# Moving the expert choice of a decoder layer's router behind slot six's row maximum, and its prefix count to slot eight

## The reference, cut to what matters

```python
x = layernorm(x + mixer(x))          # gated causal convolution with a linear scan over time
x = layernorm(x + attention(x, ctx)) # cross attention, 16 heads of 16 dims
x = layernorm(x + experts(x))        # top-1 router, 8 experts, capacity 640
# in experts, over all 4096 tokens t:
probs = softmax(t @ Wr);  idx = argmax(probs);  pmax = max(probs)
onehot = one_hot(idx, 8)
pos = sum(cumsum(onehot, axis=0) * onehot, -1) - 1
kept = pos < 640
flat = idx * 640 + minimum(pos, 639)
# kept tokens go to row `flat` of their expert's block, through relu(. @ W1) @ W2,
# and are scaled by pmax; the others stay as they are
```

## Time and profile before

| | |
|---|---|
| median of 3 runs | 869.91 us (869.25 to 873.31) |
| profiled execution | 871.27 us, span 869.5 us |
| TensorE matmul busy | 800.4 us, 92% |
| VectorE busy | 609.1 us, 70% |
| ScalarE busy | 400.6 us, 46% |
| GpSimd busy | 353.1 us, 41% |
| slices of the span at 0.9 or more of TensorE's full clock | 34 of 40 |

### The profile page before, as it was taken

How to read it: one execution, slowest core, us unless ns; L and a number is a source line. 1 busy time by engine, 2 the same in 40 slices (tenths; PEclk the granted TensorE clock), 3 DMA queues, 4 the chain that set the end, 5 groups by cost and what they waited for, 6 DMA issues and landing times. The chain is left out here.

```text
span 869.5 us, 16600 instructions
## 1 busy us (share of the span) xinstructions
PE 800.4 (92%) x5754; PEld 628.8 (72%) x5754; DVE 609.1 (70%) x1456; ACT 400.6 (46%) x644; POOL 353.1 (41%) x292
## 2 busy tenths in 40 slices
PE   8998987889998999999999999885899999999995
PEld 6776765556666767676666666544899999999994
DVE  5889883455788888888888887645266666666754
ACT  5665652135555655555655556452334234423420
POOL 1332442323255444455544453215331454255335
PEclk9999998689999999999999999897899999999999
DMA  4101931454454445465445444131512432343201
GB/s 135 49 27 48 289 106 45 140 152 130 123 169 154 115 148 159 137 172 156 124 135 174 125 143 147 56 116 44 169 51 91 129 120 86 107 146 98 79 1 49
DMA packets 76081, 100.93 MB, mean 116 GB/s; under 512 B 11065, under 2 KB 63522, under 8 KB 76024
## 3 DMA queue, kind: packets, MB, share of 16 engines
q1 hardware_dynamic: 72568, 92.06, 35.2%
q0 software_dynamic: 3456, 8.13, 2.6%
HBM read 65.47 MB, written 35.74 MB: 116 GB/s over the span
## 5 line engine op out<-in xcount | busy, mean ns | idle before, releaser
L1303 DVE TENSOR_REDUCE nmax<-ps_m 128x4 f32<-128x1024 f32 x128 | 156.6, 1224 | 49.7 <-PE ps_m L881 41.8
L1101 ACT ACTIVATE pt<-ps_a 128x1024 f32<-128x1024 f32 x128 | 131.8, 1030 | 76.6 <-PE ps_a L891 51.9
L1576 ACT ACTIVATE hid<-ps_h 128x640 fp32r<-128x640 f32 x64 | 45.2, 706 | 147.1 <-PE ps_h L1504 147.1
L1504 PE MATMUL ps_h<-xt,w_hi 128*128 128x320 f32 x512 | 101.5, 321 | 1.0 <-DVE xt L1591 1.0
L1686 POOL DMA_INDIRECT out_rows<-gated,token x40 | 50.2, 1254 | 91.4 <-issue 91.4
L1641 DVE SCALAR_TENSOR_TENSOR hid<-ps_h,hid 128x640 fp32r<-128x640 f32 x64 | 52.8, 825 | 49.2 <-ACT hid L1576 48.7
L881 PE MATMUL ps_m<-kst,qst 48*128 48x256 f32 x512 | 66.4, 338 | 19.8 <-DVE nmax L1303 15.8
L757 POOL TENSOR_TENSOR half<-kq,half 128x512 fp32r<-128x512 f32 x32 | 41.7, 1302 | 103.2 <-ACT half L1067 103.2
L1504 PEld LDWEIGHTS ps_h<-xt,w_hi 128*128 128x128 f32 x512 | 80.6, 193 | 4.1 <-DVE hid L1641 2.8
L1518 PE MATMUL ps_y<-w,hid 128*128 128x512 f32 x320 | 80.3, 393 | 0.8 <-DVE gated L1659 0.8
L881 PEld LDWEIGHTS ps_m<-kst,qst 48*128 48x128 f32 x512 | 39.6, 191 | 52.8 <-issue 25.8
(11 more groups left out here) (211 smaller groups left out, 1617.2 us busy)
## 6 DMA issues: line engine op xcount, KB each, us to landing
halves_dram<-half SPq DMA_DIRECT2D x64, 256.0 KB, 2.5
gated<-in_w SPq DMA_DIRECT2D x16, 1024.0 KB, 5.3
kst<-halves_dram SPq DMA_DIRECT2D x64, 128.0 KB, 2.6
qst<-halves_dram SPq DMA_DIRECT2D x64, 128.0 KB, 2.9
rows_dram<-blank SPq DMA_DIRECT2D x1, 5160.0 KB, 21.0
gated<-rows_dram SPq DMA_DIRECT2D x7, 645.0 KB, 4.1
x_raw<-in_x_t SPq DMA_DIRECT2D x8, 512.0 KB, 4.0
xres<-in_x SPq DMA_DIRECT2D x16, 256.0 KB, 4.1
```

The lines of the kernel that those rows point to most:

```text
L1101: nc.scalar.activation(pt[:, k % 4].rearrange("p s t q -> p (s t q)"), ps_a[:].rearrange("p s t q -> p (s t q)"), ACT.Exp).then_inc(s["exp ...
L1303: nc.vector.tensor_reduce(nmax[:, q, :, :, h // 2].rearrange("p t s -> p s t"), ps_m[:], AX.X, ALU.max, negate=True).then_inc(s["max_done" ...
L1504: mm = pe.matmul(ps_h[:, f % 2, c2, 0:HC], w1[a][:, p, k, f * P:(f + 1) * P], xt[:, b, p, k, c2 * HC:(c2 + 1) * HC], start=(n == 0 and k = ...
L1576: nc.scalar.activation(hid[:, HI, f, :].rearrange("p (c n) -> p c n", c=2), ps_h[:, f % 2, :, 0:HC], ACT.Relu).then_inc(s["hid_hi"], 1)
```

## The change

VectorE's `top_of` and `hot_of` move from slot 5 to slot 6, which puts them behind the maximum of slot six. TensorE's `count` moves from slot 7 to slot 8, where it stands behind that slot's `scores` and `scores_t` and ahead of `weigh`. `picked` and y keep their place in slot 7 of VectorE's list, ahead of slot eight's maximum. ScalarE's, GpSimd's and SyncE's lists are untouched.

```diff
--- before.py
+++ after.py
@@ -970,6 +970,8 @@
                     maxima_rows(n - 2, p)
                 if h == 12 and on(n, -1) and not (isinstance(n, int) and n < 0):
                     mixer_out(n + 1, 1)
+                if h == 8 and on(n, 4):
+                    count(n - 4)
                 j, head, lag = behind(n, h, WL)
                 if head % PV == PV - 1 and on(n, lag):
                     weigh(j, p if lag == 2 else q, head // PV)
@@ -991,8 +993,6 @@
                 if h == 6 and on(n, 0):
                     queries(n, 0)
                     queries(n, 1)
-                if h == 7 and on(n, 4):
-                    count(n - 4)
                 if h in (8, 10) and on(n, 3):
                     sums_by_query(n - 3, (h - 8) // 2)
                 if h in (8, 9) and on(n, 1):
@@ -1308,9 +1308,9 @@
                     kept_stats(n - 4, p)
                 if h == 3 and on(n, 4):
                     kept_var(rc, n - 4)
-                if h == 5 and on(n, 4):
+                if h == 6 and on(n, 4):
                     top_of(n - 4)
-                if h == 5 and on(n, 4):
+                if h == 6 and on(n, 4):
                     hot_of(rc, n - 4)
                 if h == 7 and on(n, 4):
                     picked(n - 4)
```

## The result

The changed kernel takes 899.91 us in the median of 4 runs (898.83 to 900.76), the kernel before 870.38 (869.25 to 873.31). The ratio is 1.033 (95% interval 1.029 to 1.036): 29.5 us slower. The forecast said slower, by 20 us, with 875 to 895 as its range, so the direction was right and the size too small.

What follows compares the result with a forecast made beforehand. TensorE was taken to bound the kernel. Late transposes in eleven steps summed to +20.2 us, taking the profiled 871.27 to 891.5; it stood 1.36 above the median, so 890 us was predicted, range 875 to 895.

Steps and rivals of the forecast that it cites:

- What bounds the kernel: Whole span: TensorE, busy for 92%, bounds it; nearly all of a 25.80 us step is its issue.
- nothing is given back later: Behind the transposes: no later wait absorbs a delay of TensorE; 1.51 us late there made a period 1.54 longer.
- Gain at slot eight, eaten by ScalarE: Slot eight's scores start 0.81 us earlier, but slot six's exponentials come late, leaving about 0.1 at weighing.
- The collision of y with GpSimd: VectorE's slot seven: GpSimd's copy catches one instruction of y, which takes 2.69 us instead of 1.67.
- The phase: GpSimd's copy comes 1.03 us behind y's start, in y's third instruction; both hang on E, so every step.
- E + 0.86: VectorE's slot seven: y starts 0.86 us behind E, the end of slot six's exponentials on ScalarE.
- gain of 0.1: TensorE at weighing: it starts at 401.61 instead of 401.70, about 0.1 us earlier.
- rival 4: VectorE's y: two of its instructions caught, taking hot 0.2 us later or more; 904 us, chance 0.06.
- +2.0: Transposes on TensorE: they come at 407.98 instead of 405.97, +2.0 us a step.
- the forecast's own course: VectorE: one instruction of y caught, then the capacity test stands 1.26 us, as n = 5 ran before; chance 0.52.
- +20.2: Sum over the kernel: +1.5 for n = 4, +0.5 for n = 5, +18.0 for n = 6 to 14, +0.2 for the last.
- n = 15 and 16 taken as 0: Last two steps, without y and residual sum: between -0.5 and +0.5 us together, taken as 0.

Runs made afterwards that it cites:

- e12: e11 with the whole choice (top_of too) behind slot six's maximum, as in the change; 869.43 us, ratio 0.997.
- e11: Kernel before with index and masks in slot six, count in slot eight, GpSimd's copy waiting for y, router's small instructions moved later; top value stays; 862.43 us.
- e2: Changed kernel with GpSimd's copy (low half of the queries) waiting for the end of y in steps 4 to 14; 882.93 us.
- e13: e11 without the wait of GpSimd's copy for y; 884.38 us, ratio 1.016.
- e9: Changed kernel with VectorE's loop over the steps written out, so without its register instructions; 899.53 us, ratio 1.032.
- e1: Changed kernel with y ahead of picked in VectorE's slot seven; 890.37 us, ratio 1.019.
- e5: Kernel before with only the choice moved to slot six, the count staying in slot seven; 893.93 us, ratio 1.024.
- e4: Kernel before with only the count moved to slot eight, the choice staying in slot five; 921.38 us, ratio 1.055.
- e3: Changed kernel with TensorE computing each half of the values twice in steps 4 to 14; 894.27 us, ratio 1.025.
- e10: Kernel before with VectorE's carry additions, placed and slotted behind slot ten's maximum and the normalization directly behind slot eight's; 867.11 us, ratio 0.994.

## Why the prediction was wrong, by its own steps

- **What bounds the kernel; nothing is given back later.** Right. TensorE's lateness at the transposes went into the period in full: 2.29 us there, 2.30 in the period of n = 10.
- **Gain at slot eight, eaten by ScalarE.** Right for ScalarE's chain, to 0.02 us in n = 10 up to the transposed scores, and shown by e12 against e11: with y spared in both, the late ntop costs 5.3 us in the eleven periods, 7.0 in the medians. The gain itself was over-priced, 0.52 us for the 0.81 of slot eight's scores. That did no harm, since what follows hangs on the exponentials: TensorE came to them later and waited 0.15 us for them in n = 10 (0.34 or 0.35 in most steps) instead of 0.6. At weighing the forecast's gain of 0.1 was a loss of 0.1.
- **The collision of y with GpSimd.** Right as a mechanism, shown from both sides: e2 and e13 differ from their partners (the changed kernel and e11) in the one wait and by 17 and 22 us. The Trainium skill, "SBUF — State Buffer", section "SBUF: two separate sides", states the exclusive lock; here the trace agrees with its rule that the later one stands to the end of the earlier one's instruction (y 2.68, 3.70 or 4.72 us for one, two or three instructions caught, about 1.02 us each).
- **The phase.** The term E + 0.86 for y's start measured E + 1.23 (417.54 - 416.31): the count's weight load is not hidden and the register instructions are no longer run ahead. The forecast leaned here on a margin of 0.2 us (1.03 behind y's start, in an instruction that began at 0.82). So rival 4's course occurred in nine of the eleven steps (two instructions of y), to which 0.06 had been given, though not for its reason: hot ended at 416.38, 0.07 later than worked out and ahead of the count. Its price was wrong as well: it added a whole instruction of GpSimd's to +2.0, but with two instructions of y caught the capacity test goes free. +2.0 a step measured +2.3 (n = 10's period). In n = 4 and n = 5 the forecast's own course came about, y 2.68 us and the capacity test 1.26 and 1.25.
- **The step that failed: the price of a late TensorE was taken as its idle time alone.** "The transposes come ... +2.0 us a step" was all that a step paid in the sum. The granted clock was read as 1.00 in the windows of before and carried over, without a word, to a kernel with some three times the idle time: 0.54 + 0.21 = 0.75 us a step in the earlier trace rows, 2.5 to 2.7 in the steady steps after but for n = 7's 3.0. The trace of before had nothing to warn of it: in n = 5 TensorE waited 1.06 and 1.20 us, and the projection behind it took 1.89 us all the same. Five steps paid another 1.6 to 1.9 us at the lower clock, 8.4 us together. The forecast's +20.2, plus 8.4, plus the under-priced late transposes (22.5 in place of 20.2, +2.3), minus the 1.5 ahead of n = 4, is 29.4 of the 29.5 measured. e9 has the forecast's own course in nine steps, with 28.0 us in those at full clock against the forecast's 27.8, and its five slow projections, 1.6 to 1.9 us each, make up most of the 9.5 us between it and 890.
- **n = 15 and 16 taken as 0.** Right: n = 15 measured +0.2, and n = 16 with all that follows it -0.2.

The Trainium skill, "TensorE: Matmul & The Clock Gate", section "HAM oscillation — how this bites in real kernels", describes a kernel that loses the clock again and again behind a recurring wait. The recurrence is what the trace shows here. The waits in the page's example are longer than any in these steps, so its rule would not have given this loss; that the clock falls behind waits as short as 2.02 and 0.29 us is what the rows show, and they decide.

Open: why the clock falls in some steps and not in others alike. In the profiled executions the falls among n = 4 to 14 go with the idle time of a steady step: none with at most 2.2 us (e11, e12, before, e2, e1), one with 2.0 in most and up to 3.3 (e13), three with 2.5 to 2.7 (e5), five with 2.4 to 2.9 (e9, the changed kernel), eleven with 3.8 in most (e4). In e3 the two steps with 2.5 us fell and the nine with 0.8 to 1.5 didn't. But e10 fell once with 0.85 us, and in the changed kernel n = 10 and n = 11 have the same waits (2.03 and 0.28, 2.02 and 0.29 us) and only n = 11 falls. e3 rules out the odd and even buffers. No run here shows how it is decided.

## What to carry to other kernels

Before an instruction is moved behind a wait, look at everything behind that wait in its queue, and at which other engine's work each will then meet; a fixed phase between two engines that hold each other up can be worth more than the wait that is removed (here 17 and 22 us against the 6 us of that wait). Move only the part that nobody else waits for: here the top value had a reader on ScalarE and stayed, the index and the masks could go. And price a stall of TensorE in two parts, the idle time and the clock at which it goes on.

## What the runs showed of the hardware

- A VectorE instruction with two SBUF operands and one of GpSimd's with two take turns by whole instructions: one of y's four (128x256) took 0.48 us alone and up to 1.50 when it stood; a bf16 addition over eight elements per partition 0.15 us or up to 1.25 us. The capacity test, with one SBUF operand (a tensor_scalar over 128x2), stood as well: 0.15 us (n = 10 of the kernel before) or up to 1.27 us. VectorE's maximum over PSUM kept 1.21 to 1.23 us beside the same GpSimd instructions.
- GpSimd's tensor_scalar over 128x256 (`twice`, two of them in 2.44 us from 398.34 before and in 2.43 from 413.53 after) held the choice's instructions by 0.2 us at most: hot's two took 0.47 us inside it before and 0.36 outside it after, the cast 0.36 us inside it after and 0.17 before.
- Register instructions of a loop (57 ns each, four at y) cost nothing visible where VectorE doesn't wait shortly ahead of them (carry to y 0.07 us in the loop of before), and about 0.2 us behind a wait (0.24 to 0.26 us in the loop of the changed kernel): y starts 2.91 to 2.94 us behind lg in most steps of the loop, 2.74 with the steps written out.
- TensorE's granted clock fell to the lower level behind waits of 2.02 and 0.29 us (changed kernel), behind 0.82 and 1.38 us (e9) and once behind 0.85 us (e10), but also stayed up behind the same waits; the eight matmuls behind it took up to 3.6 us for 1.9.
